# Attention kernel: four pairs of key blocks joined by accumulating DMAs, row sums inverted in turned form

## The chip, the cores and the metric

One core of one Trainium2 chip runs the whole kernel. The metric is the device time of one execution in microseconds. TensorE multiplies matrices into PSUM, VectorE and ScalarE do elementwise work, GpSimd (POOL) and SyncE (SP) mostly issue and fill here, and 16 DMA engines move data between HBM and SBUF.

## What is computed

A decoder layer with three parts on x of 2 x 2048 tokens x 512: self-attention with 16 heads of 32, cross-attention on 77 context rows, and a feed-forward part with rounded weights and activations, each followed by a layer norm. The change lies in the first:

```python
qkv = jnp.einsum('bnd,ed->bne', x, w_qkv)
q, k, v = jnp.split(qkv, 3, axis=-1)
dots = jnp.einsum('bhnd,bhmd->bhnm', q, k) * SCALE
attn = jax.nn.softmax(dots, axis=-1)
out = jnp.einsum('bhnm,bhmd->bhnd', attn, v)
```

## The kernel before

The stages run one after the other: project (queries, keys, values, to HBM), attend, mix (output projection and cross-attention), and two for the feed-forward part. `attend` is called a second time under a condition that does not hold for these inputs; each engine skips it then.

**Loops.** `attend` goes over 8 iterations (4 groups of 4 heads, 2 batches), in each over 4 chunks of 512 queries (`CPB`), in each over 16 blocks of 128 keys (`KB`): 32 chunks. For a block and two heads (a pair) TensorE makes scores, 128 keys x 1024 (`score`, L801), three score tiles being in flight; ScalarE takes the exponential into half of a tile `probs` of 128 x 2048 (L698), and there are 8 such tiles (`P_SLOTS`), block n using tile n modulo 8; TensorE multiplies the tile with the values and adds it up in `mixed_ps` over the 16 blocks (L842). In the order of TensorE's queue, block n has the scores of exponentials 2n+3 and 2n+4 ahead of its own mixing.

**Row sums.** The softmax's divisor is the sum of all 16 tiles over their 128 partitions. VectorE adds the tiles of blocks 0 to 13 elementwise into `dve_sum` (L762, 13 adds). The last two, the raw blocks, stay in their tiles. After block 2 of the next chunk (`SUMS_AT`), TensorE sums the two raw tiles and `dve_sum` over the partitions with a matrix of ones (`finish` of the tensor block, L815: 3 tiles x 4 heads, each product in two passes, 24 matmuls, four heads side by side), into the PSUM bank that held the mixture, which VectorE has copied away by then (`gather`, L711). Each sum stands 32 times there, once for each row of its head.

**Finish.** After its third add of the next chunk (`FINISH_AT` is 3), VectorE's `finish` inverts the sums (L720, 128 x 512), multiplies (L725), splits the product in two parts for the output (L728, L731) and adds the inverses to a running tile (L729), whose maximum says at the end whether the second attention is needed. SP stores the parts (L642).

**Waits.** ScalarE may write a tile of `probs` again when its last reader is through: an add of VectorE (L694), or for a raw tile the sums (L692). SP loads the next chunk's queries when a chunk starts, and in every fourth chunk the next iteration's keys and values in four pieces, the first of which it issues when block 3 is mixed (L665). GpSimd only fills the two raw tiles with ones at the start.

## Time and profile before

| what | value |
|---|---|
| time, median of 3 runs | 2044.34 us (2042.05 to 2046.21) |
| the profiled execution | 2044.68 us, span 2042.9 us |
| mean granted clock of TensorE | 0.965 |
| busy over the span | PE 94%, DVE 81%, ACT 70%, POOL 5% |
| DMA | 221.70 MB, mean 109 GB/s |
| exponentials (L698) | 1024 x 1022 ns on ACT |
| adds (L762) | 384 x 2292 ns and 32 x 2284 ns on DVE |

Times are in microseconds from the start of the span unless ns is written. PE is TensorE's matmuls and PEld its weight loads, DVE is VectorE, ACT ScalarE, POOL GpSimd; SPq is SP's queue. The rows in order of time have start, busy time, engine, line, operation, written and read tiles, shapes and count, and in brackets the idle time of that engine before and what ended it; several alike are one row. Matmuls overlap, so their distance says more than their length.

### The profile page before, as it was taken

What the parts mean: (1) busy time and instruction counts of PE and PEld (TensorE: products, weight loads), DVE (VectorE), ACT (ScalarE), POOL (GpSimd) and SP (SyncE); (2) the same over time, 40 slices, a digit from 0 to 9 for tenths busy, and PEclk for the clock granted to TensorE, in tenths of its full rate; (3) what the DMA queues carried; (4) which work ended last, traced back from release to release, by engine and by line L of the source; (5) the groups of instructions that cost most, each with busy time, mean ns of one, the idle gap of its engine ahead of it and who ended that gap; (6) DMA issues with size and microseconds to landing.
All of it is one profiled execution on the core that took longest, in us unless ns stands there. A gap on an engine that the chain in (4) does not pass through costs nothing. (4 is left out here: it accounts for less than half of the span.)

```text
span 2042.9 us, 31283 instructions
## 1 busy us (share of the span) xinstructions
PE 1910.2 (94%) x10398; PEld 936.1 (46%) x10398; DVE 1656.2 (81%) x1461; ACT 1422.3 (70%) x1593; POOL 106.5 (5%) x67
## 2 busy tenths in 40 slices
PE   8999996999999999999999999999958998699786
PEld 6777772333333333333333333333325775344332
DVE  4434436999999999999999999999963776688687
ACT  5444535888888888888888888888843655465465
POOL 0000000000000000000000000000002210000164
PEclk9999997999999999999999999999988997799898
DMA  7655647124133132142151151150146530123174
GB/s 274 231 191 212 223 178 164 43 54 99 36 78 84 37 87 65 37 96 58 35 120 42 35 118 37 42 120 26 42 106 208 174 126 18 43 128 170 63 281 160
DMA packets 114410, 221.70 MB, mean 109 GB/s; under 512 B 9576, under 2 KB 28136, under 8 KB 112764
## 3 DMA queue, kind: packets, MB, share of 16 engines
q1 hardware_dynamic: 110332, 212.23, 34.6%
q10 hardware_dynamic: 3968, 7.86, 1.0%
q8 instruction: 85, 1.39, 0.3%
q14 instruction: 25, 0.20, 0.0%
HBM read 134.61 MB, written 85.46 MB: 108 GB/s over the span
## 5 line engine op out<-in xcount | busy, mean ns | idle before, releaser
L698 ACT ACTIVATE probs<-scores 128x1024 f32<-128x1024 f32 x1024 | 993.5, 1022 | 187.8 <-PE scores L801 187.7
L762 DVE TENSOR_TENSOR dve_sum<-dve_sum,probs 128x2048 f32<-128x2048 f32 x384 | 880.0, 2292 | 12.0
L801 PE MATMUL scores<-q_stack,k_stack 97*128 97x512 f32 x2054 | 617.0, 422 | 26.8 <-DMA v_group<-v_scratch 18.2
L801 PEld LDWEIGHTS scores<-q_stack,k_stack 97*128 97x128 f32 x2054 | 345.7, 188 | 503.4 <-ACT probs L698 415.0
L842 PE MATMUL mixed_ps<-probs,v_group 128*32 128x512 f32 x4096 | 545.5, 605 | 0.0
L842 PEld LDWEIGHTS mixed_ps<-probs,v_group 128*32 128x32 f32 x4096 | 80.5, 108 | 188.7 <-issue 188.7
L333 DVE TENSOR_TENSOR parts<-proj_ps,parts 128x512 fp32r<-128x512 f32 x64 | 44.1, 690 | 94.4 <-ACT parts L263 94.4
L1194 PE MATMUL mix_y_ps<-w_out_parts,mix_o_in 128*128 128x512 f32 x384 | 98.5, 411 | 22.3 <-DMA mix_o_in<-o_scratch 22.3
L720 DVE RECIPROCAL row_inverse<-mixed_ps 128x512 f32<-128x512 f32 x33 | 110.8, 3357 | 6.2 <-PE mixed_ps L815 5.0
L411 PE MATMUL proj_ps<-x_hi,qkv_hi 128*128 128x512 f32 x256 | 102.2, 399 | 9.9 <-DVE qkv_lo L322 9.9
L1710 PE MATMUL down_y_ps<-down_t,down_ints 128*128 128x512 bf16 x352 | 85.2, 407 | 21.9 <-DVE down_ints L1619 21.9
L411 PE MATMUL proj_ps<-x_lo,qkv_hi 128*128 128x512 f32 x256 | 101.0, 395 | 0.0
L411 PE MATMUL proj_ps<-x_hi,qkv_lo 128*128 128x512 f32 x256 | 100.9, 394 | 0.0
L1383 ACT ACTIVATE up_gated<-up_gate_ps,up_gate_scale 128x512 f32<-128x512 f32 x88 | 59.5, 686 | 59.4 <-PE up_gate_ps L1466 36.0
L1466 PE MATMUL up_gate_ps<-up_ints_t,gate_up_t 128*128 128x512 bf16 x352 | 91.2, 382 | 1.7 <-ACT up_ints_t L1369 1.7
L1194 PEld LDWEIGHTS mix_y_ps<-w_out_parts,mix_o_in 128*128 128x128 f32 x384 | 73.0, 193 | 41.1 <-DMA mix_o_in<-o_scratch 22.8
L1466 PE MATMUL up_up_ps<-up_ints_t,gate_up_t 128*128 128x512 bf16 x352 | 90.9, 381 | 0.0
L1423 DVE SCALAR_TENSOR_TENSOR h<-up_up_ps,up_up_scale,up_gated 128x512 f32<-128x512 f32 x88 | 63.5, 745 | 30.2 <-ACT up_gated L1383 24.2
L259 ACT ACTIVATE squares<-proj_ps 128x512 bf16<-128x512 f32 x64 | 38.3, 598 | 70.9 <-PE proj_ps L411 70.9
L762 DVE TENSOR_TENSOR dve_sum<-probs 128x2048 f32<-128x2048 f32 x32 | 73.1, 2284 | 8.4 <-ACT probs L698 8.4
L1710 PEld LDWEIGHTS down_y_ps<-down_t,down_ints 128*128 128x128 bf16 x352 | 36.0, 104 | 70.7 <-issue 35.3
L815 PE MATMUL mixed_ps<-probs,ones 128*32 128x512 f32 x528 | 62.7, 592 | 1.9 <-DVE mixed L711 1.9
(184 smaller groups left out, 1715.6 us busy)
## 6 DMA issues: line engine op xcount, KB each, us to landing
k_stack<-k_scratch SPq DMA_DIRECT2D x108, 256.0 KB
q_stack<-q_scratch SPq DMA_DIRECT2D x99, 256.0 KB
o_scratch<-out_parts SPq DMA_DIRECT2D x33, 512.0 KB, 3.0
h_scratch<-h SPq DMA_DIRECT2D x6, 2816.0 KB, 8.1
h<-h_scratch SPq DMA_DIRECT2D x6, 2816.0 KB, 10.9
k_scratch<-parts SPq DMA_DIRECT2D x32, 512.0 KB, 6.6
q_scratch<-parts SPq DMA_DIRECT2D x32, 512.0 KB, 2.7
mix_o_in<-o_scratch SPq DMA_DIRECT2D x32, 512.0 KB, 7.9
```

Of the source, the lines that this page charges most:

```text
L411: last = nc.tensor.matmul(bank[:], lhs, rhs, start=t == 0, stop=t == len(terms) - 1)
L698: nc.scalar.activation(probs[n % P_SLOTS][:, pair * 2 * CH:(pair + 1) * 2 * CH], scores[e % S_SLOTS][:], ACT.Exp, scale=SCALE).then_inc(pr ...
L720: nc.vector.reciprocal(inverse[:], mixed_ps[u][:]).then_inc(sums_read, 1)
L762: nc.vector.tensor_tensor(total[:], first[:], probs[n % P_SLOTS][:], ALU.add).then_inc(dve_added, 1)
L801: last = nc.tensor.matmul(scores[e % S_SLOTS][:, j * CH:(j + 1) * CH], k_stack[:, h, k * P:(k + 1) * P], q_stack[c % 2][:, h, :], start=Tr ...
L815: last = nc.tensor.matmul(mixed_ps[u][j * HD:(j + 1) * HD, :], keep.ones[:, 0:HD], part[:, j * CH:(j + 1) * CH], start=p == 0, stop=p == l ...
L842: last = nc.tensor.matmul(mixed_ps[c % 2][j * HD:(j + 1) * HD, :], v_group[:, k, j * HD:(j + 1) * HD], probs[n % P_SLOTS][:, j * CH:(j + 1 ...
L1194: last = nc.tensor.matmul(y_ps[t % 2][:], o_in[u][:, k, a, t * P:(t + 1) * P], (w_hi, w_lo)[b][:, k, :], start=m == 0, stop=m == len(terms ...
L1383: nc.scalar.activation(gated[t % 2][:], gate_ps[t % BANKS][:], ACT.Silu, scale=gate_scale[:, t:t + 1]).then_inc(gate_out, 1)
L1423: nc.vector.scalar_tensor_tensor(h[u][:, t, :], up_ps[t % BANKS][:], up_scale[:, t:t + 1], gated[t % 2][:], ALU.mult, ALU.mult).then_inc(h ...
L1466: last = nc.tensor.matmul(acc[t % BANKS][:], keep.gate_up_t[:, k, first + t * P:first + (t + 1) * P], ints_t[u][:, k, :], start=k == 0, st ...
L1710: last = nc.tensor.matmul(y_ps[u][t][:], ints[u][:, r, t * P:(t + 1) * P], keep.down_t[:, r, :], start=r == 0, stop=r == IT - 1)
```

## The change

Each chunk's blocks 0 to 7 are joined in four pairs: when the odd block k (1, 3, 5, 7) is mixed, GpSimd issues a DMA that adds the tile of block k-1 to that of block k, in SBUF, 1 MB (`accum_op`). No block stays raw. VectorE adds the four joined tiles and those of blocks 8 to 15: 12 tiles, 11 adds, in the order 1, 3, 8, 5, 9, 10, 7, 11 to 15. TensorE sums `dve_sum` alone, 8 matmuls instead of 24, and after block 5 instead of block 2. VectorE's finish stands ahead of all adds of its chunk (`FINISH_AT` 0), and inverts in another form: a transpose of 32 x 32 squares (the 32 copies of a sum go side by side), the reciprocal of one column of each of 16 squares, a copy of it to all 32, and a transpose back. The running inverses are 16 columns instead of 512. ScalarE waits for the DMA where it writes the tile of an even block below 8 again, and for an add elsewhere: block 9 writes tile 1 and waits for the first add, that of tiles 1 and 3.

```diff
--- before.py
+++ after.py
@@ -559,11 +559,14 @@
     PIECES = 4
     KPP = KB // PIECES
 
-    RAW_BLOCKS = range(KB - 2, KB)
-    ADDS = KB - len(RAW_BLOCKS) - 1
+    MERGED = (1, 3, 5, 7)
+
+    ORDER = (1, 3, 8, 5, 9, 10, 7, 11, 12, 13, 14, 15)
+    ADDS = len(ORDER) - 1
+    COLS = CH // HD
     W_SLOT = 4
-    SUMS_AT = 2
-    FINISH_AT = 3
+    SUMS_AT = 5
+    FINISH_AT = 0
@@ -581,8 +584,11 @@
...
+        turned = sb("sums_turned", [P, COLS, HD], F32)
+        turned_inverse = sb("turned_inverse", [P, COLS], F32)
         inverse = sb("row_inverse", [P, CH], F32)
-        inverses = sb("inverses", [P, CH], F32)
+        inverses = sb("inverses", [P, COLS], F32)
...
@@ -688,10 +697,10 @@
 
                                 before = n - P_SLOTS
                                 chunk, block_in = it * CPB + before // KB, before % KB
-                                if block_in in RAW_BLOCKS:
-                                    act.wait_ge(sums_done, chunk + 3)
+                                if block_in + 1 in MERGED:
+                                    act.wait_ge(dma_added[MERGED.index(block_in + 1)], 16 * (chunk + 1))
                                 else:
-                                    act.wait_ge(dve_added, (chunk + 1) * ADDS + max(block_in, 1))
+                                    act.wait_ge(dve_added, (chunk + 1) * ADDS + max(ORDER.index(block_in), 1))
                                 for pair in range(PAIRS):
                                     e = n * PAIRS + pair
                                     act.wait_ge(scores_done, 1 + it * EXPS + e + 1)
@@ -716,17 +725,25 @@
                         f = it * CPB + c
                         v.wait_ge(sums_done, 1 + f + 1)
 
+                        v.wait_ge(inverted, 3 * f)
+                        nc.vector.transpose(turned[:].rearrange("p c j -> p (c j)"), mixed_ps[u][:]).then_inc(sums_read, 1)
+                        v.wait_ge(sums_read, 1 + f + 1)
                         v.wait_ge(inverses_done, 1 + f)
-                        nc.vector.reciprocal(inverse[:], mixed_ps[u][:]).then_inc(sums_read, 1)
+                        nc.vector.reciprocal(turned_inverse[:], turned[:, :, 0]).then_inc(inverted, 1)
+                        v.wait_ge(inverted, 3 * f + 1)
+                        nc.vector.tensor_copy(turned[:], turned_inverse[:].unsqueeze(2).broadcast_to([P, COLS, HD])).then_inc(inverted, 1)
+                        nc.vector.tensor_tensor(inverses[:], inverses[:], turned_inverse[:], ALU.add).then_inc(inverses_done, 1)
+                        v.wait_ge(inverted, 3 * f + 2)
+                        v.wait_ge(normal_done, 1 + f)
+                        nc.vector.transpose(inverse[:], turned[:].rearrange("p c j -> p (c j)")).then_inc(inverted, 1)
                         v.wait_ge(mixed_copied, f + 1)
-                        v.wait_ge(sums_read, 1 + f + 1)
+                        v.wait_ge(inverted, 3 * f + 3)
 
                         v.wait_ge(lo_done, 2 + f - 1)
                         nc.vector.tensor_tensor(normal[u][:], mixed[:], inverse[:], ALU.mult).then_inc(normal_done, 1)
                         v.wait_ge(normal_done, 1 + f + 1)
                         v.wait_ge(stored[u], 1 + it * (16 * CPB // 2) + 16 * (c // 2))
                         nc.vector.tensor_copy(out_parts[u][:, 0, :], normal[u][:]).then_inc(hi_done, 1)
-                        nc.vector.tensor_tensor(inverses[:], inverses[:], inverse[:], ALU.add).then_inc(inverses_done, 1)
                         v.wait_ge(hi_done, f + 1)
                         nc.vector.tensor_tensor(out_parts[u][:, 1, :], normal[u][:], out_parts[u][:, 0, :].bitcast(F32),
                                                 ALU.subtract).then_inc(lo_done, 1)
@@ -747,17 +764,21 @@
                         for c in range(CPB):
                             total = dve_sum[c % 2]
                             gather(it, c)
-                            for a in range(ADDS):
-                                n = c * KB + a + 1
+                            for a, k in enumerate(ORDER):
                                 if a == FINISH_AT:
                                     finish(it, c)
-                                v.wait_ge(probs_done, (it + 1) * EXPS + (n + 1) * PAIRS)
+                                n = c * KB + k
+                                if k in MERGED:
+                                    v.wait_ge(dma_added[MERGED.index(k)], 16 * (it * CPB + c + 1))
+                                else:
+                                    v.wait_ge(probs_done, (it + 1) * EXPS + (n + 1) * PAIRS)
                                 if a == 0:
 
                                     v.wait_ge(sums_done, 1 + it * CPB + c)
-                                    first = probs[(n - 1) % P_SLOTS]
-                                else:
-                                    v.wait_ge(dve_added, (it * CPB + c + 1) * ADDS + a)
+                                    first = probs[n % P_SLOTS]
+                                    continue
+                                if a >= 2:
+                                    v.wait_ge(dve_added, (it * CPB + c + 1) * ADDS + a - 1)
                                     first = total
                                 nc.vector.tensor_tensor(total[:], first[:], probs[n % P_SLOTS][:], ALU.add).then_inc(dve_added, 1)
...
@@ -777,9 +798,13 @@
             @block.gpsimd
             def _(pool):
                 with only_if(pool, keep, again):
-
-                    for k in RAW_BLOCKS:
-                        nc.gpsimd.memset(probs[k % P_SLOTS][:], 1.0).then_inc(raw_filled, 1)
+                    with pool.Fori(0, ITERS) as it:
+                        for c in range(CPB):
+                            for at, k in enumerate(MERGED):
+                                n = c * KB + k
+                                pool.wait_ge(mixed_done, (it + 1) * BLOCKS + n + 1)
+                                pool.sem_inc(may_add, 1)
+                                nc.gpsimd.dma_start(probs[n % P_SLOTS][:], probs[(n - 1) % P_SLOTS][:], accum_op=ALU.add).then_inc(dma_added[at], 16)
 
...
@@ -806,14 +831,10 @@
 
                         u = (c + 1) % 2
                         pe.wait_ge(mixed_copied, it * CPB + c + 1)
-                        pe.wait_ge(raw_filled, len(RAW_BLOCKS))
-                        parts = [probs[k % P_SLOTS] for k in RAW_BLOCKS] + [dve_sum[u]]
-                        for p, part in enumerate(parts):
-                            if part is dve_sum[u]:
-                                pe.wait_ge(dve_added, (it * CPB + c + 1) * ADDS)
-                            for j in range(HPG):
-                                last = nc.tensor.matmul(mixed_ps[u][j * HD:(j + 1) * HD, :], keep.ones[:, 0:HD], part[:, j * CH:(j + 1) * CH],
-                                                        start=p == 0, stop=p == len(parts) - 1)
+                        pe.wait_ge(dve_added, (it * CPB + c + 1) * ADDS)
+                        for j in range(HPG):
+                            last = nc.tensor.matmul(mixed_ps[u][j * HD:(j + 1) * HD, :], keep.ones[:, 0:HD], dve_sum[u][:, j * CH:(j + 1) * CH],
+                                                    start=True, stop=True)
                         last.then_inc(sums_done, 1)
```

## Rows read from the trace of the kernel before

**Rows 1.** Busy time by stretch: one chunk, and the attention (first row: columns)
```profile
core 0: us, PE busy (x) PEld busy (x) DVE busy (x) ACT busy (x) POOL busy (x), PEclk, DMA share, GB/s
704.66:741.17 36.51, 36.51 (x217) 14.07 (x218) 35.89 (x19) 31.05 (x32) 0.00 (x0) 1.00 0.14 37
322.50:1507.00 1184.50, 1175.54 (x6926) 451.39 (x6926) 1151.80 (x610) 1002.51 (x1031) 0.00 (x0) 1.00 0.29 68
```

**Rows 2.** The page's costliest groups: line, engine, operation, shapes, count, busy, mean, idle before
```profile
L762 DVE TENSOR_TENSOR dve_sum<-dve_sum,probs 128x2048 f32<-128x2048 f32 x384 | 880.0, 2292 | 12.0
...
L815 PE MATMUL mixed_ps<-probs,ones 128*32 128x512 f32 x528 | 62.7, 592 | 1.9 <-DVE mixed L711 1.9
```

**Rows 3.** Instructions in order of time, all engines, around one chunk's sums
```profile
700.95 0.16 PEld L842 LDWEIGHTS mixed_ps<-probs,v_group 128*32 128x32 f32 x8 [0.37 <-issue]
...
701.41 0.13 PEld L815 LDWEIGHTS mixed_ps<-probs,ones 128*32 128x32 f32 x4 [0.30 <-issue]
...
703.55 0.13 PEld L815 LDWEIGHTS mixed_ps<-dve_sum,ones 128*32 128x32 f32 x4 [0.30 <-issue]
...
704.52 0.77 PEld L801 LDWEIGHTS scores<-q_stack,k_stack 97*128 97x128 f32 x4 [0.84 <-issue]
...
704.66 3.36 DVE L720 RECIPROCAL row_inverse<-mixed_ps 128x512 f32<-128x512 f32 x1
```

**Rows 4.** The same view, a later stretch: one block between the sums
```profile
713.78 1.94 ACT L698 ACTIVATE probs<-scores 128x1024 f32<-128x1024 f32 x2 [0.18 <-PE scores L801]
...
714.14 0.16 PEld L842 LDWEIGHTS mixed_ps<-probs,v_group 128*32 128x32 f32 x8 [0.37 <-issue]
...
716.26 0.16 PEld L842 LDWEIGHTS mixed_ps<-probs,v_group 128*32 128x32 f32 x8 [0.37 <-issue]
```

**Rows 5.** The same view through narrow windows, single instructions of that block
```profile
713.36 0.86 PE L801 MATMUL scores<-q_stack,k_stack 97*128 97x512 f32 x3
...
714.71 1.02 ACT L698 ACTIVATE probs<-scores 128x1024 f32<-128x1024 f32 x1
```

**Rows 6.** The same view: VectorE through one finish and to the next
```profile
708.11 0.69 DVE L725 TENSOR_TENSOR normal<-mixed,row_inverse 128x512 f32<-128x512 f32 x1
...
708.92 0.43 DVE L728 CAST out_parts<-normal 128x512 fp32r<-128x512 f32 x1
...
709.87 0.68 DVE L731 TENSOR_TENSOR out_parts<-normal,out_parts 128x512 fp32r<-128x512 f32 x1
...
710.47 23.22 DVE L762 TENSOR_TENSOR dve_sum<-dve_sum,probs 128x2048 f32<-128x2048 f32 x10
...
741.17 3.36 DVE L720 RECIPROCAL row_inverse<-mixed_ps 128x512 f32<-128x512 f32 x1
```

**Rows 7.** VectorE's groups by line and shape over the whole span
```profile
L711 DVE COPY mixed<-mixed_ps 128x512 f32<-128x512 f32 x33 | 22.5, 683 | 0.0
...
L728 DVE CAST out_parts<-normal 128x512 fp32r<-128x512 f32 x33 | 14.1, 427 | 2.6
...
L1100 DVE RECIPROCAL mix_inverse<-mix_total 128x4 f32<-128x4 f32 x9 | 1.6, 179 | 0.3
```

**Rows 8.** DMA issues of the page: size, median us from issue to landing
```profile
o_scratch<-out_parts SPq DMA_DIRECT2D x33, 512.0 KB, 3.0
...
v_scratch<-values SPq DMA_DIRECT2D x32, 256.0 KB, 2.0
...
x_raw<-in_w_qkv_t SPq DMA_DIRECT2D x1, 1024.0 KB, 11.8
```

**Rows 9.** DMA share in tenths, 40 slices of 743 to 752 us
```profile
DMA  0000011397999989999999999994000000000000
```

**Rows 10.** Instructions in order of time at the end of the attention
```profile
1505.53 0.16 PEld L842 LDWEIGHTS mixed_ps<-probs,v_group 128*32 128x32 f32 x8 [0.36 <-issue]
...
1507.78 0.69 DVE L711 COPY mixed<-mixed_ps 128x512 f32<-128x512 f32 x1
...
1511.37 3.36 DVE L720 RECIPROCAL row_inverse<-mixed_ps 128x512 f32<-128x512 f32 x1 [2.90 <-PE mixed_ps L815]
```

More of the change, by code:

```diff
@@ L598, in attend @@
         mixed_done = sem("mixed_done")
-        dve_added, raw_filled = sem("dve_added"), sem("raw_filled")
+        dve_added, may_add = sem("dve_added"), sem("may_add")
+        dma_added = [sem(f"dma_added{k}") for k in MERGED]
         mixed_copied = sem("mixed_copied")
         sums_done, sums_read, normal_done = sem("sums_done"), sem("sums_read"), sem("normal_done")
+        inverted = sem("inverted")
         inverses_done, hi_done, lo_done = sem("inverses_done"), sem("out_hi_done"), sem("out_lo_done")
-        col_done, row_done, all_done = sem("inverses_col_done"), sem("inverses_row_done"), sem("inverses_all_done")
-        most_done = sem("inverses_most_done")
-        w_in, w_hi_done, w_lo_done = sem("w_out_in"), sem("w_out_hi_done"), sem("w_out_lo_done")
+        if not again:
+            col_done, row_done, all_done = sem("inverses_col_done"), sem("inverses_row_done"), sem("inverses_all_done")
+            most_done = sem("inverses_most_done")
+            w_in, w_hi_done, w_lo_done = sem("w_out_in"), sem("w_out_hi_done"), sem("w_out_lo_done")
         stored = [sem(f"stored{u}") for u in range(2)]
```

## The prediction

> **What bounds the kernel now.** I read the busy times by stretch first, because the change touches only the attention. There, from 322.5 to 1507 us, TensorE is busy 1175.5 of 1184.5 us and VectorE 1151.8, ScalarE 1002.5; in one chunk, from one row-sum inversion to the next, 36.51 us long, they are busy 36.51, 35.89 and 31.05 us [rows 1]. There are 32 such chunks. So two engines are full at once, and a gain must relieve both.
>
> The view in order of time tells what fills TensorE. A block of 128 keys goes by every 2.12 us (714.14 to 716.26) [rows 4], and the chunk's row sums come on top: from the first weight load of a block's mixing at 700.95 to the next scores at 704.52 are 3.57 us [rows 3]. In them lie the sums, 24 matmuls, issued as six fours; the first four's weights load at 701.41 and the last four's at 703.55, five steps, so 0.43 us a four [rows 3], and 0.99 is left for the mixing itself. 16 x 2.12 + 6 x 0.43 = 36.5, the whole chunk.
>
> ScalarE trails TensorE: it waits 0.18 us in each block for scores, and its two exponentials take 1.94 [rows 4]. The pair at 713.78 and 714.71 [rows 5] are the second of block n+1 and the first of block n+2, where block n is the one whose mixing starts at 714.14: the scores are issued three ahead. Hence ScalarE asks for the tile of block n+2 as early as 0.57 us after the mixing of block n starts. This matters most below.
>
> **Part by part.**
>
> *TensorE, removed.* The 16 matmuls on the two raw blocks are four of the six fours: 4 x 0.43 = 1.71 us a chunk. If TensorE alone decided, a chunk would take 36.51 - 1.71 = 34.80 us; 32 chunks give 54.8 us.
>
> *VectorE, removed and added.* Adds go from 13 to 11 a chunk at 2.29 us each [rows 2]; with their step, 23.22 us for ten [rows 6], I use 2.33. The finish of the previous chunk was 704.66 to 710.47 = 5.81 us [rows 3, 6], its reciprocal of 512 columns 3.36 of it [rows 3]. The new one has no row for the transpose. Its bounds: 0.43, what a conversion of that shape takes, and 0.68, a copy of it out of PSUM [rows 7]; I take 0.68, as it reads the same PSUM tile or writes as many columns, for each of the two. The reciprocal of 16 columns lies between 0.18 for four columns [rows 7] and that plus 12 x 6.5 ns (3.36 us / 512), 0.26; I take 0.25. The broadcast copy lies between 0.43 and 0.68 [rows 7]; I take 0.43, it stays in SBUF. A dependent step starts some 0.1 us after its predecessor (708.11 + 0.69 to 708.92) [rows 6]. So: transpose 0.78, reciprocal 0.35, copy and the small add into the running inverses 0.58, transpose 0.78, product to conversion 0.81, conversion 0.55, subtraction to the next add 0.60 (709.87 to 710.47) [rows 6]: 4.45 us, say 4.5; between 3.9 (all moves at 0.43) and 4.8. VectorE's work falls to 11 x 2.33 + 0.6 + 4.5 = 30.7 us a chunk: it is no longer full.
>
> *The order, moved.* The sums go from after block 2 to after block 5, and the finish goes ahead of all adds of its chunk. The first add now joins tiles 1 and 3 and is the only thing that frees tile 1, which block 9 needs. So there is a new chain. Counted from the start of block 5's mixing: finish starts after 704.66 - 700.95 - 1.71 = 2.00 us [rows 3]; finish 4.5; first add 2.4 with its handover; the two exponentials of block 9, 1.94 [rows 4] and 0.1 to hand over; the second pair of the following scores up to the mixing, 714.14 - 713.36 = 0.78 [rows 4, 5]. Mixing of block 9 starts 11.72 us after that of block 5. TensorE by itself would be there after 4 x 2.12 + 0.86 = 9.34. It stands still for 2.38 us a chunk. Behind the waiting exponential are all later ones, then scores 21 and 22, then the mixing; nothing else covers. Does the time come back? The chain closes: block 9 to the next chunk's block 5 is 12 x 2.12 = 25.44 us of full TensorE, and the finish hangs on that. Period 11.72 + 25.44 = 37.16 us; before 36.51. So the removal's 1.71 is more than eaten, +0.65 a chunk, 32 x 0.65 = 21 us. The later tiles have room: tile 3 goes free with tile 1, tile 5 two adds on, tile 7 five adds on, 11.7 us after the first, when ScalarE asks for it six blocks, 12.7 us, later than for tile 1. VectorE ends its adds about 5.5 us into the next chunk, and TensorE wants the copied mixture and the total only at 11, so the gather and the total are covered.
>
> *GpSimd and the DMA queues.* Two 1 MB fills at the start go; they ran beside other work. New are four accumulating DMAs a chunk of 1 MB, 128 in all. No row shows one. Lower bound: from 256 KB in 2.0 us and 512 KB in 3.0 us [rows 8], a plain MB would land in 5.0 and move for 4. Upper bound: the slowest MB of the trace, 11.8 us [rows 8], among other loads. An add must read two tiles; if the moving part doubles, 9.0. I take 7 us, between the plain line and the doubled one, with both ends kept. What does that cost? The one for blocks 2 and 3 is issued when block 3 is mixed, 1.2 us after its start, and the first add starts 4.24 + 6.5 = 10.74 after it by the chain: it may take 9.6 us unseen. Those for even tiles (0, 2, 4, 6) have 11 us and more before ScalarE asks. Their load: 0.29 of 36.51 us [rows 1], 10.6, is taken by the present traffic, and 4 x 5 comes: 31 of 37 us, so the queues hold, up to 6.6 us of moving time each. In every fourth chunk the key and value loads are issued in the same instant as the one for block 3, and keep the engines busy for 24 of 40 slices, 5.4 us [rows 9]. Shared fully, 7 becomes 12 and adds 2.4; not shared 0. I take 1 us in each of 8, +8 us.
>
> The Trainium skill, Collectives: The Full Stack, section on the bandwidth ceiling, says that a reducing transfer goes at half a copy's rate because it makes two reads. The trace has no such transfer. By that rule, with the fit in DMA: Bandwidth & Descriptors, section Anatomy of one DMA (2.0 us plus size over 436 GB/s), the estimate would be 6.8 us, and this sum would stay as it is.
>
> *The end.* The last chunk's adds run until 7.8 us after block 15's mixing starts, and copy, sums and wait bring the last finish to 9.6; before it was 1511.37 - 1505.53 = 5.84 [rows 10]. The finish is 1.3 shorter, the last maximum over 16 instead of 512 columns 0.5: +2 us.
>
> *Sum.* The profiled execution took 2044.7 us (span 2042.9; the median of the runs shown is 2044.3). 2044.7 + 21 + 8 + 2 = **2076 us**.
>
> **The rivals.**
>
> *The accumulating DMA is late.* If it lands later than 9.6 us after issue, it and not the finish holds the first add. From block 3: 1.2 + L + 2.4 + 2.04 + 0.78, then 10 blocks, 21.2: a chunk is 27.6 + L. L = 12 gives 39.6 and 2044.7 + 32 x 3.1 + 2 = 2146 us; beyond 6.6 us of moving time the queues themselves are full. For it: the double read, the slowest MB at 11.8 [rows 8], the collision [rows 9]. Against: 512 KB in 3.0 us.
> A rule that speaks for it stands in the Trainium skill, SBUF: State Buffer, section Who interferes with whom: while VectorE moves data in a two-port mode, GpSimd can't write the descriptors of its DMA. Here VectorE is busy most of the time, but such moves are short; by the rule alone I would expect well under 1 us. No row shows it.
>
> *The finish is short: faster.* It decides in the stretch between sums and first add. Below 3.85 us instead of 4.5 the chunk is shorter than 36.51; at 2.1 TensorE is the bound again, and all 54.8 come back: 1992 us. All three moves at 0.43 give 3.9 to 4.0: 36.6 us, with the end and no collision 2050. What could be wrong further is a handover of 0.1 that is hidden. For it: VectorE's total work falls by over 5 us. Against: seven dependent steps, each with a row of its kind.
>
> *TensorE's clock falls in the new standstill.* Granted clock is 1.00 in the attention [rows 1]; at half clock the blocks after each standstill cost double for a while. One block each chunk: +2.1 x 32, 2143 us. The present trace has no standstill of this length inside the attention that would tell.
>
> **How the numbers follow.** Forecast case 0.62 (2055 to 2105, without the collision or with all of it and a finish of 4.8). Late DMA 0.20 (2105 to 2250). Clock 0.03. Finish near 3.9, no collision: 0.07, around 2045. Faster 0.08, from 1992 to 2040. A difference of 0.2%, about 4 us, is what a measurement of this kernel can tell. So faster 0.08, same 0.07, slower 0.85. The range leaves out the faster case and the top of the late DMA: 2042 to 2160.
>
> **What would show it.** The chunk period, from one PSUM transpose to the next: 37.2, and not 34.8. ScalarE idle about 3 us before block 9's exponentials (asked for at 0.86 + 2 x 2.12 + 0.57 = 5.7, free at 8.9), released by the add of VectorE; TensorE idle 2.4 us ahead of the scores that follow; VectorE idle 4 to 5 us before the transpose, waiting for the sums. DMAs that land in 7 us, and none ahead of the first add. Wrong if the first add waits for a DMA instead, if the new finish takes under 4 us, or if block 9 finds its tile free.

## The result, and the profile after

The changed kernel takes 2176.02 us (median of its runs, 2173.49 to 2180.53), the kernel before beside it 2045.28: a ratio of 1.0642, 95% interval 1.0618 to 1.0666. The forecast was 2076, with a range of 2042 to 2160, so the result lies 16 us above it. The sign was right; instead of +31 us it is +131.

First the stretches. Four neighbouring chunks, each one period long (the cuts lie 0.15 us behind the first mixing of a block 0), and the attention; columns as in [rows 1]:

```profile
core 0: us, PE busy (x) PEld busy (x) DVE busy (x) ACT busy (x) POOL busy (x), PEclk, DMA share, GB/s
819.24:861.89 42.65, 39.74 (x204) 14.78 (x204) 28.41 (x20) 30.94 (x33) 3.44 (x4) 0.88 0.72 155
861.89:900.06 38.17, 36.69 (x204) 13.99 (x201) 27.70 (x21) 30.93 (x33) 3.44 (x4) 0.96 0.68 145
900.06:938.32 38.26, 36.69 (x204) 13.90 (x200) 30.22 (x21) 30.92 (x33) 3.44 (x4) 0.96 0.67 144
938.32:985.89 47.57, 38.09 (x204) 14.56 (x201) 34.30 (x23) 32.60 (x34) 3.47 (x4) 0.90 0.88 188
322.50:1640.00 1317.50, 1200.19 (x6411) 453.02 (x6409) 952.53 (x641) 998.17 (x1031) 110.23 (x128) 0.93 0.75 162
```

A chunk took 36.51 us at clock 1.00 [rows 1] (38.0 in the mean where the loop over iterations closes). Now no engine is full and the four chunks of an iteration differ: 42.65, 38.17, 38.26, 47.57. The forecast was 37.16 for each. The DMA share went from 0.29 over the attention to 0.75. And the granted clock, 1.00 before, is 0.88 to 0.96: TensorE spends part of each of these chunks at 1.2 GHz.

The second of them in order of time, around the sums and block 9:

```profile
872.79 0.13 PEld L836 LDWEIGHTS mixed_ps<-dve_sum,ones 128*32 128x32 f32 x4 [0.30 <-issue]
...
874.42 0.72 DVE L729 STREAM_TRANSPOSE sums_turned<-mixed_ps 128x512 f32<-128x512 f32 x1 [9.42 <-PE mixed_ps L836]
...
875.17 0.25 DVE L732 RECIPROCAL turned_inverse<-sums_turned 128x16 f32<-128x16 f32 x1
...
875.46 0.43 DVE L734 COPY sums_turned<-turned_inverse 128x512 f32<-128x512 f32 x1
...
875.92 0.71 DVE L738 STREAM_TRANSPOSE row_inverse<-sums_turned 128x512 f32<-128x512 f32 x1
...
878.47 2.28 DVE L783 TENSOR_TENSOR dve_sum<-probs 128x2048 f32<-128x2048 f32 x1
...
880.86 4.69 ACT L707 ACTIVATE probs<-scores 128x1024 f32<-128x1024 f32 x5 [2.75 <-DVE dve_sum L783]
881.94 0.30 PEld L826 LDWEIGHTS scores<-q_stack,k_stack 97*128 97x128 f32 x2 [2.21 <-ACT probs L707]
...
881.94 0.73 PE L826 MATMUL scores<-q_stack,k_stack 97*128 97x512 f32 x2 [1.30 <-ACT probs L707]
...
884.99 1.35 PEld L826 LDWEIGHTS scores<-q_stack,k_stack 97*128 97x128 f32 x4 [1.32 <-ACT probs L707]
```

Here the chain of the forecast stands link for link. VectorE waits for the sums; the finish takes 874.42 to 878.47, 4.05 us; the first add follows at once, so nothing but the finish holds it; ScalarE has stood 2.75 us for block 9's tile and goes when the add is done (880.86); TensorE stands for the slot of the scores: no weight load for 2.21 us and no matmul for 1.30 us. (A weight load also waits 0.84 us where nothing stands still [rows 3], so the second figure is the standstill.) What the forecast lacked is the last row: four weight loads of scores take 1.35 us, where [rows 3] has 0.77. TensorE's granted clock has gone to 1.2 GHz, about 2 us after it resumed; the two loads at 881.94 still take 0.30 us. The stretches around it:

```profile
866.00:876.00 10.00, 10.00 (x65) 3.71 (x64) 1.51 (x5) 8.41 (x10) 2.11 (x3) 1.00 0.96 193
876.00:882.00 6.00, 4.70 (x29) 1.72 (x25) 5.86 (x6) 3.06 (x4) 0.86 (x1) 1.00 1.01 202
882.00:888.00 6.00, 5.82 (x24) 2.05 (x24) 5.90 (x4) 5.30 (x6) 0.00 (x0) 0.72 1.05 258
888.00:898.00 10.00, 10.00 (x60) 4.15 (x60) 9.33 (x5) 8.54 (x10) 0.00 (x0) 1.00 0.18 39
```

Clock 1.00 up to the standstill, 0.72 as a mean of the 6 us that begin with TensorE's return, 1.00 again after.

In the first and the fourth chunk of an iteration it is another wait. The first adds there, with the issue of the DMA for blocks 2 and 3 that each needs, and the loop's end, in order of time:

```profile
828.72 0.86 POOL L807 DMA_DIRECT2D probs<-probs  x1 [3.39 <-PE mixed_ps L863]
...
838.84 2.29 DVE L783 TENSOR_TENSOR dve_sum<-probs 128x2048 f32<-128x2048 f32 x1 [1.24 <-DMA probs<-probs]
...
946.20 0.87 POOL L807 DMA_DIRECT2D probs<-probs  x1 [2.64 <-PE mixed_ps L863]
...
957.84 2.29 DVE L783 TENSOR_TENSOR dve_sum<-probs 128x2048 f32<-128x2048 f32 x1 [2.85 <-DMA probs<-probs]
...
983.73 1.36 PEld L826 LDWEIGHTS scores<-q_stack,k_stack 97*128 97x128 f32 x4 [6.13 <-issue]
```

The first add starts 10.1 us after that issue in the one and 11.6 in the other, and has waited 1.24 and 2.85 us for the DMA. At the loop's end TensorE makes no weight load for 6.13 us and no matmul for 5.2, with nothing to wait for that the profile shows, and comes back at the low clock (1.36 us).

The page's rows of the accumulating DMAs: their queue with its packets, MB and share of 16 engines' span, and the median from issue to landing. Between them is the queue that brings instructions, of which more below:

```profile
q0 software_dynamic: 18432, 134.23, 30.6%
...
q8 instruction: 85, 1.39, 0.3%
...
probs<-probs POOLq DMA_DIRECT2D x128, 1024.0 KB, 9.4
```

30.6% of 2178.4 us by 128 is 5.2 us of moving each, where 5 was taken; the landing is at 9.4 in the median, where 7 was taken for one alone.

The starts of all 512 blocks' mixings give a balance by place. It is the sum over chunks of one kind, in us; "first" is the very first chunk, the last has 15 block steps; the columns to the right are experiments 1, 9 and 10 below.

| chunks | before | after | no DMA | no DMA, filled | after, filled |
|---|---|---|---|---|---|
| first | 36.5 | 49.2 | 38.7 | 36.8 | 43.8 |
| first of an iteration, 7 | 255.6 | 293.1 | 268.2 | 257.2 | 277.5 |
| second, 8 | 292.1 | 300.8 | 308.5 | 293.2 | 295.2 |
| third, 8 | 292.1 | 304.6 | 296.8 | 293.8 | 294.0 |
| fourth, 7 | 265.9 | 322.0 | 282.9 | 266.8 | 312.9 |
| last | 34.6 | 39.8 | 36.3 | 34.7 | 40.0 |
| sum | 1176.8 | 1309.5 | 1231.4 | 1182.5 | 1263.4 |

So 132.7 of the 135.5 us between the two spans lie in these chunks.

The granted clock over the same chunks (the number before the DMA share), one row each for the changed kernel and for experiments 1, 9 and 10 in this order; in the kernel before it is 1.00:

```profile
325.90:1635.30 1309.40, 1195.69 (x6389) 451.70 (x6388) 945.72 (x638) 995.63 (x1028) 110.23 (x128) 0.93 0.75 162
326.10:1557.50 1231.40, 1168.62 (x6390) 442.00 (x6389) 945.62 (x639) 995.01 (x1028) 0.00 (x0) 0.96 0.27 64
327.70:1510.20 1182.50, 1173.98 (x6901) 445.84 (x6900) 942.57 (x638) 991.95 (x1028) 0.00 (x0) 1.00 0.28 66
329.20:1592.60 1263.40, 1206.63 (x6903) 454.65 (x6902) 945.30 (x639) 991.06 (x1028) 110.32 (x128) 0.98 0.78 168
```

In experiment 9 the clock never falls there; in 10 it still falls 15 times, for 61 us together.

### The profile page after: what moved, and what is told of

Read it like the earlier page. It is cut to its first block and busy times, and to the rows that moved or that the text cites. A ratio compares the mean times of both kernels' runs of the same rounds, so it can differ in the third digit from the quotient of the medians.

```text
span 2178.4 us, 30509 instructions
## 1 busy us (share of the span) xinstructions
PE 1930.4 (89%) x9844; PEld 937.0 (43%) x9870; DVE 1455.5 (67%) x1496; ACT 1418.7 (65%) x1593; POOL 213.3 (10%) x193
## 3 DMA queue, kind: packets, MB, share of 16 engines
q0 software_dynamic: 18432, 134.23, 30.6%
q10 hardware_dynamic: 3968, 7.86, 0.9%
q8 instruction: 85, 1.39, 0.3%
## 5 line engine op out<-in xcount | busy, mean ns | idle before, releaser
L826 PE MATMUL scores<-q_stack,k_stack 97*128 97x512 f32 x2054 | 662.6, 444 | 132.2 <-ACT probs L707 84.4
L783 DVE TENSOR_TENSOR dve_sum<-dve_sum,probs 128x2048 f32<-128x2048 f32 x320 | 733.6, 2292 | 26.6 <-DMA probs<-probs 16.3
L826 PEld LDWEIGHTS scores<-q_stack,k_stack 97*128 97x128 f32 x2054 | 363.5, 199 | 659.3 <-ACT probs L707 560.4
L863 PE MATMUL mixed_ps<-probs,v_group 128*32 128x512 f32 x4096 | 579.5, 639 | 0.0
L807 POOL DMA_DIRECT2D probs<-probs x128 | 110.2, 861 | 1502.2 <-PE mixed_ps L863 1468.8
L729 DVE STREAM_TRANSPOSE sums_turned<-mixed_ps 128x512 f32<-128x512 f32 x33 | 23.7, 717 | 296.9 <-PE mixed_ps L836 296.9
L783 DVE TENSOR_TENSOR dve_sum<-probs 128x2048 f32<-128x2048 f32 x32 | 73.2, 2288 | 35.4 <-DMA probs<-probs 35.4
L1731 PEld LDWEIGHTS down_y_ps<-down_t,down_ints 128*128 128x128 bf16 x352 | 35.4, 102 | 72.4 <-issue 36.1
## 6 DMA issues: line engine op xcount, KB each, us to landing
h<-h_scratch SPq DMA_DIRECT2D x6, 2816.0 KB, 10.9
```

The lines of the kernel that those rows point to most:

```text
L783: nc.vector.tensor_tensor(total[:], first[:], probs[n % P_SLOTS][:], ALU.add).then_inc(dve_added, 1)
L807: nc.gpsimd.dma_start(probs[n % P_SLOTS][:], probs[(n - 1) % P_SLOTS][:], accum_op=ALU.add).then_inc(dma_added[at], 16)
L826: last = nc.tensor.matmul(scores[e % S_SLOTS][:, j * CH:(j + 1) * CH], k_stack[:, h, k * P:(k + 1) * P], q_stack[c % 2][:, h, :], start=Tr ...
L863: last = nc.tensor.matmul(mixed_ps[c % 2][j * HD:(j + 1) * HD, :], v_group[:, k, j * HD:(j + 1) * HD], probs[n % P_SLOTS][:, j * CH:(j + 1 ...
L1731: last = nc.tensor.matmul(y_ps[u][t][:], ints[u][:, r, t * P:(t + 1) * P], keep.down_t[:, r, :], start=r == 0, stop=r == IT - 1)
```

## The experiments

All are edits of the changed kernel except 4. Times are medians, ratios against the kernel before (2043.8 to 2044.4 us) on the same chip with 95% intervals. Two questions: what the accumulating DMAs cost and what the chain costs (1 to 5), and what of the chain is clock (9, 10); 6, 7, 8 and 11 look for a better use of the same parts.

**1. No accumulating DMA.** It leaves out the adding of tiles 0, 2, 4, 6.

```diff
-                                    act.wait_ge(dma_added[MERGED.index(block_in + 1)], 16 * (chunk + 1))
+                                    act.wait_ge(mixed_done, (it + 1) * BLOCKS + before + 1)
...
+                                v.wait_ge(probs_done, (it + 1) * EXPS + (n + 1) * PAIRS)
...
+                                if a == 1:
+                                    nc.vector.scalar_tensor_tensor(total[:], first[:], 1e-20, probs[n % P_SLOTS][:], ALU.add, ALU.add).then_inc(dve_added, 1)
+                                    continue
...
-                                nc.gpsimd.dma_start(probs[n % P_SLOTS][:], probs[(n - 1) % P_SLOTS][:], accum_op=ALU.add).then_inc(dma_added[at], 16)
```

> The changed kernel without its 128 accumulating DMAs: the tiles of blocks 0, 2, 4 and 6 are left out of the row sums, VectorE and ScalarE wait for no DMA, and the first add of a chunk puts in 1e-20 so that no sum is zero. Order, place of the sums and of the finish are those of the change. Theory A (the chain of prediction: sums after block 5, finish, first add, tile 1, scores) says that the wait before block 9 stays in every chunk: full-clock chunks of 36.6 us, and where TensorE's clock falls in the standstill 38.1, so 32 x 1.6 = 51 us over the kernel before, about 2096 us; TensorE's loop branch is back from 5.8 to 7.5 at the 3.4 to 3.9 us of before. Theory B (the landing of the accumulating DMAs is the whole loss) says 36.6 us a chunk or less with no fallen clock, 2050 us or less.

Measured: 2098.11 us, 1.0279 (1.0253 to 1.0305). The DMAs cost 77.9 us, the rest of the change 53.7. (The first add, in its other form, takes 2284 ns; it was 2288.) Two neighbouring chunks of it, and TensorE behind the standstill of each, in order of time:

```profile
675.58:713.76 38.18, 36.70 (x204) 13.85 (x200) 29.64 (x21) 30.95 (x33) 0.00 (x0) 0.96 0.13 35
713.76:750.49 36.73, 35.16 (x204) 13.45 (x200) 28.19 (x20) 30.84 (x33) 0.00 (x0) 1.00 0.14 36
```

```profile
695.55 0.30 PEld L820 LDWEIGHTS scores<-q_stack,k_stack 97*128 97x128 f32 x2 [2.21 <-ACT probs L707]
...
695.55 0.73 PE L820 MATMUL scores<-q_stack,k_stack 97*128 97x512 f32 x2 [1.30 <-ACT probs L707]
...
699.43 1.00 PEld L820 LDWEIGHTS scores<-q_stack,k_stack 97*128 97x128 f32 x4 [1.66 <-ACT probs L707]
...
733.81 0.30 PEld L820 LDWEIGHTS scores<-q_stack,k_stack 97*128 97x128 f32 x2 [2.30 <-ACT probs L707]
...
733.81 0.73 PE L820 MATMUL scores<-q_stack,k_stack 97*128 97x512 f32 x2 [1.39 <-ACT probs L707]
...
736.38 0.77 PEld L820 LDWEIGHTS scores<-q_stack,k_stack 97*128 97x128 f32 x4 [0.84 <-ACT probs L707]
```

Nearly the same standstill, 1.30 and 1.39 us without a matmul; behind the shorter one the clock falls and behind the longer one it stays. The difference is 38.18 - 36.73 = 1.45 us. In the whole run the clock falls so in 26 of the 32 chunks: in all first, second and fourth ones, in two of the eight third ones. That gave the theory for experiment 9.

**2. No DMA, sums two blocks earlier.** It leaves out the same work.

```diff
-    SUMS_AT = 5
+    SUMS_AT = 3
```

> As the run before, and the sums made after block 3 instead of block 5. The same part is left out. Theory A: the first add ends 4.2 us earlier, before ScalarE asks for tile 1, TensorE never stands still, a chunk is 34.8 us, the clock stays, 2044 - 54.8 + 2 = about 1992 us. Theory B does not care for the place of the sums: the same time as the run before. Theory C (with the removed matmuls another bound of the same size shows, such as ScalarE) says more than 2020 us.

Measured: 2004.5 us, 0.9808 (0.9791 to 0.9824). A second chunk:

```profile
645.40:680.20 34.80, 34.80 (x204) 13.54 (x200) 29.68 (x21) 31.02 (x33) 0.00 (x0) 1.00 0.15 39
```

34.80 us, TensorE full at clock 1.00: to the digit what the 16 removed matmuls should leave. The chain is what eats the gain. First chunks (36.0 to 36.4 in five of seven) and fourth ones (37.1) keep it 12 us above the 1992 expected. Here TensorE makes no matmul for 1.9 to 2.0 us at each loop's end; behind five of the seven the clock falls, and those five first chunks are the long ones, the other two take 34.8.

**3. Sums two blocks earlier, DMAs kept.** The same line alone.

> The changed kernel with the sums after block 3 instead of block 5, nothing else. Theory A alone would give back all but the collisions, below 2060 us. Theory A with B (finish and the landing of the DMA for blocks 2 and 3 end within 0.6 us of one another in undisturbed chunks, and the DMA is last by itself in the first and the fourth chunk of an iteration) says 0.6 us in half the chunks, about 10 us: 2166 us, and the first add then waits for the DMA in every chunk.

Measured: 2158.71 us, 1.0567 (1.0539 to 1.0595), 7 us under the expected 2166 and 17 under the changed kernel. A second chunk, and the first add in it:

```profile
698.73:735.34 36.61, 35.50 (x204) 13.39 (x203) 27.36 (x20) 30.46 (x33) 3.44 (x4) 1.00 0.71 153
```

```profile
714.82 2.29 DVE L783 TENSOR_TENSOR dve_sum<-probs 128x2048 f32<-128x2048 f32 x1 [3.52 <-DMA probs<-probs]
```

The finish ends 3.5 us before the add can start: with the finish out of the way the DMA for blocks 2 and 3 holds the add, only 0.6 us earlier (first add 16.1 us after the chunk's start, 16.7 with the finish last). The two limits lay that close together, and an earlier finish alone is worth little.

**4. The kernel before, with the new finish alone.** Sums and finish stay where they were, raw blocks too.

```diff
-                        nc.vector.reciprocal(inverse[:], mixed_ps[u][:]).then_inc(sums_read, 1)
+                        nc.vector.transpose(turned[:].rearrange("p c j -> p (c j)"), mixed_ps[u][:]).then_inc(sums_read, 1)
...
+                        nc.vector.transpose(inverse[:], turned[:].rearrange("p c j -> p (c j)")).then_inc(inverted, 1)
```

> The kernel before with only the turned inversion of the change (4.0 instead of 5.8 us of VectorE for a finish). If TensorE is the bound of the kernel before by itself, the time stays at 2044 within 3 us and VectorE gets 1.8 us of idle time a chunk. If VectorE's full queue sets the period and TensorE is only stretched to it, a chunk gets 1.8 us shorter: 1988 us.

Measured: 2040.25 us, 0.9982 (0.9973 to 0.9992); its chunks are 36.51 us as before. VectorE was full [rows 1] but not what set the chunk: TensorE was.

**5. Keys and values not loaded again.** Every iteration works on the first group's.

```diff
-                                    load_kv(ng, nb, piece)
...
-                            pe.wait_ge(kv_in[k // KPP], (it + 1) * KV_UP)
+                            pe.wait_ge(kv_in[k // KPP], KV_UP)
```

> The changed kernel without the reloads of keys and values in every fourth chunk: all iterations use the keys and values of the first, a part left out. The collision theory says that in the fourth chunk the DMA for blocks 2 and 3 then lands as in the second, the first add starts at 16.8 us instead of 19.5 from the chunk's start, and TensorE's loop branch falls from 5.8 to 7.5 toward 4.3 us: the fourth chunk goes from 46.0 to about 40.5 us, 7 times 5.5, and something of the first chunk (its DMA runs beside the query loads too), so 2125 to 2140 us. If the accumulating DMAs are late by their own number alone (5.1 us of moving every 4.2 us), the fourth chunk stays above 44 us and the time at 2170 us.

Measured: 2167.77 us, 1.0593 (1.0567 to 1.0619). A miss: the collision with these loads is worth 8 us, not 36 to 51. Fourth chunks still take 44.5 (46.0 in the changed kernel). That is the time of the other theory, but not its mechanism: second chunks have as many DMAs and theirs aren't late. A DMA's landing is the last of 16 events, one for each engine. For the pair (2, 3), from issue, in the mean: in fourth chunks of the changed kernel 15 have come at 10.38 us and the last at 11.31, so beside the loads all engines are late; without the loads it is 8.02 and 9.69. In second chunks it is 7.86 and 7.87, and in first ones of the changed kernel 7.81 and 9.79. So the loads do slow the DMA, by 1.6 us, and something else holds up a single engine.

**6. Two pairs only, (0, 1) and (2, 3).**

```diff
-    MERGED = (1, 3, 5, 7)
+    MERGED = (1, 3)
...
-    ORDER = (1, 3, 8, 5, 9, 10, 7, 11, 12, 13, 14, 15)
+    ORDER = (1, 4, 5, 3, 6, 7, 8, 9, 10, 11, 12, 13, 14, 15)
...
-    SUMS_AT = 5
-    FINISH_AT = 0
+    SUMS_AT = 6
+    FINISH_AT = 5
```

> Two pairs instead of four (blocks 0 and 1, 2 and 3), so 13 adds and two accumulating DMAs a chunk; adds in the order 1, 4, 5, 3, 6 to 15, sums after block 6, finish ahead of the sixth tile. TensorE has its 8 sum matmuls as in the change. VectorE needs 13 x 2.33 + 0.6 + 4.0 = 34.9 us a chunk, TensorE 34.8. The first add (tiles 1 and 4) waits neither for the finish nor for the second DMA and ends near 13 us, before ScalarE asks for tile 1 at 16.3. Theory A with B: no standstill, 34.9 us a chunk, about 2004.5 (the run without DMAs and with early sums) plus 3 for a longer loop branch plus 3 for VectorE: 2010 us. If DMA traffic of this kind costs by itself, wherever it stands, a third to half of its 130 us stays: above 2045.

Measured: 2049.97 us, 1.0025 (1.0015 to 1.0036), a miss for 2010; the other theory had said above 2045. But the second and third chunks are at 34.8 to 35.4 (one at 36.0), as meant, so the traffic doesn't cost wherever it stands. Fourth chunks take 40.8: the second DMA lands there 11.6 us after issue, and the loop's end, block 15 to the next block 0, takes 6.2 us, of which 3.4 to 4.1 are without a matmul.

**7. Three pairs, without (4, 5); the finish after seven tiles.**

The added lines:

```diff
+    MERGED = (1, 3, 7)
+    ORDER = (1, 4, 5, 3, 8, 9, 7, 10, 11, 12, 13, 14, 15)
...
+    FINISH_AT = 7
```

> Three pairs (0 and 1, 2 and 3, 6 and 7), 12 adds, order 1, 4, 5, 3, 8, 9, 7, 10 to 15, sums after block 5, finish ahead of the eighth tile. VectorE 32.6 us a chunk, so it has 2.2 to spare, and three DMAs. Theory A with B: 34.8 us a chunk but for the fourth of an iteration, where the DMA for blocks 6 and 7 lands some 3 us late (12.9 us after issue as in the change): 2010 to 2025 us, not better than two pairs.

Measured: 2071.21 us, 1.0128 (1.0111 to 1.0146), a miss like 6: second and third chunks 34.8 to 35.7, first ones up to 40.3 (the pair (0, 1) lands 12.8 us after issue there), fourth ones 40.4.

**8. Two pairs apart, (0, 1) and (4, 5).**

The added lines:

```diff
+    MERGED = (1, 5)
+    ORDER = (2, 3, 1, 6, 7, 5, 8, 9, 10, 11, 12, 13, 14, 15)
...
+    SUMS_AT = 4
+    FINISH_AT = 3
```

> Two pairs again, but blocks 0 and 1 and blocks 4 and 5, 8.5 us apart, so that neither DMA queues behind the other; order 2, 3, 1, 6, 7, 5, 8 to 15, sums after block 4, finish ahead of the fourth tile. The same 13 adds. Theory A with B: as with the pairs 0, 1 and 2, 3 within 5 us, 2010 us, since a landing that nobody waits for costs nothing; if the queueing of one accumulate behind the other costs, it is the faster of the two by more than 5 us.

Measured: 2025.68 us, 0.9912 (0.9893 to 0.9931): the fastest with the whole sum in it, faster than both kernels. As many DMAs as in 6, 24 us less, 21 of them in fourth chunks, which take 37.8. Three things differ from 6, and no run takes them apart: the two DMAs overlap only in the very first chunk and in one other (issued 8.6 to 10.2 us apart), each starts an add that has others ahead of it, and sums and finish stand earlier. Over the expected 2010 it is by first and fourth chunks again.

**9. Experiment 1 with a filled standstill.** After block 8 TensorE does 16 matmuls of the sums once more, on a result that is never read.

```diff
+                                if k == 8:
+                                    pe.wait_ge(sums_read, 1 + it * CPB + c + 1)
+                                    for fill in range(2):
+                                        for j in range(HPG):
+                                            nc.tensor.matmul(mixed_ps[(c + 1) % 2][j * HD:(j + 1) * HD, :], keep.ones[:, 0:HD], dve_sum[(c + 1) % 2][:, j * CH:(j + 1) * CH],
+                                                             start=True, stop=True)
```

> The run without accumulating DMAs (2098 us), and after each block 8 TensorE makes 16 more matmuls, the row sums once more and twice over, 1.7 us, into the PSUM bank whose sums VectorE has read by then. They stand in the 1.8 us in which TensorE otherwise waits for the scores' slot, so by themselves they cost nothing. Theory A' (half of what the change costs without DMAs is TensorE's clock, which falls after the standstill): the clock stays at full level in the chunks, all go at 36.6 us instead of 38.2 in most, 25 to 30 chunks x 1.5 = about 40 us: 2050 to 2062 us. If the slow blocks after the standstill have another cause (ScalarE catching up, weights), the time stays at 2098, or rises by what of the fill isn't hidden.

Measured: 2055.83 us, 1.0052 (1.0035 to 1.0068), 42.3 us under experiment 1 with more work for TensorE. A second chunk:

```profile
661.15:697.80 36.65, 36.65 (x220) 13.98 (x224) 29.69 (x21) 30.83 (x33) 0.00 (x0) 1.00 0.14 37
```

All first to third chunks take 36.6 to 36.8 at clock 1.00. The 38.2 of experiment 1 are gone; block 9 still starts 11.18 to 11.28 us after block 5. The clock is shown as a cause, and 36.65 is the chain's own period. The fill does one thing more: at the loop's ends TensorE is without a matmul for 1.1 to 1.3 us, as in the kernel before, and not for 1.75 to 2.16 as in experiment 1. That is about 5 of the 42 us, and nothing here says why.

**10. The changed kernel with the same fill.**

> The changed kernel with the same fill. Theory A' with B: in the second and third chunks of an iteration 36.6 us instead of 38.2; in the first and fourth the standstill is 3 to 5 us long and the fill covers 1.7 of it, so the clock may still fall there. 2130 to 2160 us. Other cause: 2176.

Measured: 2137.84 us, 1.0453 (1.0430 to 1.0476): 38.2 us under the changed kernel. The longest of the second chunks (they take 36.7 to 37.1):

```profile
689.44:726.59 37.15, 36.97 (x220) 13.93 (x223) 28.58 (x21) 30.45 (x33) 3.44 (x4) 1.00 0.70 150
```

**11. Three pairs, spaced: (0, 1), (4, 5), (6, 7).**

The added lines:

```diff
+    MERGED = (1, 5, 7)
+    ORDER = (2, 3, 1, 5, 8, 9, 7, 10, 11, 12, 13, 14, 15)
...
+    FINISH_AT = 3
```

> The version with pairs 0, 1 and 4, 5 (2025.7 us) with a third pair, 6 and 7: 12 adds, VectorE 32.6 us a chunk instead of 34.9, order 2, 3, 1, 5, 8, 9, 7, 10 to 15, sums after block 5. If VectorE's full queue is what is left there (second chunks of 35.3 on average against 34.8), it gains up to 0.5 us a chunk: 2010 to 2020 us. If late DMAs in the fourth chunk decide, it loses: above 2030 us.

Measured: 2041.12 us, 0.9986 (0.9977 to 0.9996). Second and third chunks 34.8, first ones 35.2, but fourth ones 41.4: the DMAs for (4, 5) and (6, 7), issued 5.1 us apart, land there 10.9 and 12.2 us after issue. So the expectation's second branch holds, above 2030: late DMAs in the fourth chunk decide between three pairs and two.

## Why the forecast was right in sign and wrong in size

**TensorE bounds the kernel before, and the removal is worth 1.71 us a chunk: right.** Experiments 4 (VectorE relieved, chunk unchanged) and 2 (34.80 us).

**The chain through the finish sets the period: right, and 0.5 us too long.** Block 9 follows block 5 by 11.18 to 11.28 us where the clock stays (forecast 11.72), the period is 36.65 (37.16). The term that was off is the finish: 4.05 us instead of 4.5, with 0.72 and 0.71 for the transposes (0.68 taken), 0.25 for the reciprocal and 0.43 for the copy as taken, and handovers of 0.03 between these steps, not 0.1 (874.42 + 0.72 to 875.17). So this step is 32 x 0.14, some 5 us, instead of 21. (By the medians experiment 9 is 12 us over the kernel before, but 7 of them lie behind the start of the last block.) The sign of the forecast was therefore partly luck: the chain that it rested on gives 5 to 12 of the 131 us.

**The clock: the step that failed first.** The forecast counted a standstill of 2.38 us (block 9 came 1.82 us behind its full-rate place, 11.18 - 9.36, and 1.30 to 1.41 of that are without a matmul) and gave a fall of the clock behind it 0.03. So the main sum had this term at nothing, with the reason that the trace of before has no standstill of this length in the attention. At the length that came about, it has seven, at the loop's ends, and the clock stays at 1.00:

```profile
PE scores L801 <- ACT probs L698: 8.6, 7, 1.5
```

Read at that place, they would have spoken for 0.03 as well, and yet in experiment 1 the clock falls behind 26 of 32 standstills of that length, and behind none of the seven of 1.75 to 2.16 us at its loop's ends. So the length of a standstill alone doesn't decide, and what does stays open. Its price as a rival, 2.1 us a chunk, was high; it is 1.45 (experiment 1). By the balance the fill gains 1309.5 - 1263.4 = 46 us with the DMAs and 1231.4 - 1182.5 = 49 without, by the medians 38 and 42. The later stages of the profiled executions differ by as much as the two ways of counting do (behind the start of the last block 538.0 us in experiment 1, 544.6 in 9).

**The DMA in most chunks: right.** 7 us was a choice between bounds of 5 and 9, so the exact hit is partly luck; where one runs alone, it is 7.0. Pair (2, 3) lands at 7.87 in second chunks and 8.27 in third ones, as it starts before the first is through (one is issued every 4.24 us and moves for 5.1). Its margin of 9.6 us was really 8.7 (issued 8.04 us after the chunk's start, first add free to start at 16.73), as the issue was later and the finish shorter than forecast. Even so the finish comes last in second and third chunks.

**The collision: the step that failed second.** 1 us in each of 8 chunks was taken, 8 us in all; it is 1263.4 - 1182.5 = 81 us by the balance, 78 to 82 by the medians (the changed kernel less 1, 10 less 9). Of the 81, 46 lie in the fourth chunks (6.6 each), 20 in the first ones of an iteration (2.9 each), 7 in the very first, 5 in the last. Part of the 81 is clock again: in 10 it still falls 15 times, 13 of them in fourth chunks, for 61 us together. By the rate of experiment 1 (49 us lost with 96 us at the low clock) that is up to 31 us, an estimate and an upper one, since the clock is partly low while TensorE stands. In the fourth chunks the first add is 2.7 us late, and the loop's end is longer: block 15 to the next block 0 took 3.3 to 3.7 us before, 5.7 to 8.3 now. The rows of the waits between 400 and 1500 us count TensorE's idle time there as follows, for the changed kernel and for experiment 8 (engine, tile and line; then total, times, longest); the kernel before has no such row:

```profile
PE scores L826 <- issue: 28.8, 7, 5.2
```

```profile
PE scores L826 <- issue: 5.4, 2, 3.0
```

The forecast named only the loads of the fourth chunk as partner, busy for 24 slices by its reading (the row shows 23). That collision exists and costs 8 us, as much as was taken; experiment 5 takes it out and leaves the other 70. It had no term for first chunks, for the very first (its pair (2, 3) lands 14.3 us after issue, in a stretch with the DMA engines full), nor for the loop's end. The rival of a late DMA had the mechanism, but in every chunk; it comes in two of four.

**The end.** +2 us was taken, on the last finish starting 9.6 us after block 15 against 5.84 [rows 10]; it starts 9.6 us after it (10.2 in experiment 9). Behind the start of the last block the span has 5.8 us more in the changed kernel, 7.3 in experiment 9 and 0.7 in experiment 1, so this term stays unresolved within the scatter of the later stages.

**The sum again**, with what was measured, against the 21 + 8 + 2 of the forecast. By the balance: chain 5.7 (9 less before), DMAs 80.9 (10 less 9), clock 46.1 (the changed kernel less 10), together 132.7. By the medians: 12, 82 and 38, together 132 for a measured 131.

**What stays open.** Why one DMA engine of 16 is late in first and fourth chunks: the page has a queue that brings instructions, 85 packets and 1.39 MB, so 16 KB a packet. In each of the seven first chunks one of them, 0.9 to 1.0 us long, moves 6.5 to 9.1 us after the issue of the DMA for (2, 3). The last of that DMA's 16 completion writes comes within 0.02 us of the packet's end in five of them and 0.7 us behind it, about one 8 KB packet, in the other two. In second chunks no such packet moves then, and the last write comes within 0.02 us of the one before it. The trace doesn't name the engines and no experiment moved such a packet, so this is argued, not shown. What makes TensorE's loop end longer isn't settled either; block 15 to the next block 0 takes 3.3 to 3.5 us in experiment 9, 3.9 to 4.3 in 1 though the clock is full there, 4.1 to 4.6 in 2, and 3.9 to 7.3 in 10. So part of it comes without any of these DMAs. With three pairs (7 and 11) it takes 2.5 to 3.6 but for one at 5.2; in 11 TensorE has stood 2.1 to 2.5 us a few blocks earlier there.

## What to carry to other kernels

A new standstill on TensorE has two prices, its own length and the blocks at the lower clock behind it. Give the fall a weight in the range and not 0.03, even where the trace has standstills of this length without one. A transfer that is off the critical path in the common chunk must be followed through the chunks where other traffic, a loop's end or the start of a stage falls in: there was the larger part of this cost. And of four pairs two, spaced so that their DMAs hardly ever overlap and with other adds ahead of each, were worth 19 us (the new finish's 4 among them), while all four cost 131.

## What the hardware showed that was not expected

- **The clock behind a short standstill.** After 1.30 to 1.41 us without a matmul TensorE went from 2.4 to 1.2 GHz in 26 of 32 chunks (experiment 1), 0.9 to 2.1 us after it had resumed, and came back a few blocks later; behind equal ones it did not, nor behind seven of 1.75 to 2.16 us in the same run. 16 matmuls in the gap, on data never used, saved 38 and 42 us of 2100.
- **An accumulating DMA within SBUF.** 1 MB lands 7.0 us after the issue, 0.86 of them GpSimd's issue; the first packet starts 1.43 us after the issue begins, its packets of 8 KB take 0.635 us in the median, eight to an engine, 5.1 us. The Trainium skill's rule in Collectives: The Full Stack (section on the bandwidth ceiling) of half a copy's rate gave an estimate of 6.8; the total of 7.0 agrees with it, while the half rate itself isn't shown, as no run has a plain copy of this shape. Of the lock in SBUF: State Buffer (Who interferes with whom) of the same skill the trace shows nothing: 127 of GpSimd's 128 issues take 0.85 to 0.88 us, among them 13 with a copy of VectorE beside them before their first packet.
- **A DMA is as late as its last engine.** In first chunks of the changed kernel 15 engines are done at 7.81 us and the last at 9.79, in the mean: 1.98 us of wait for one sixteenth of the data.
